# Feature-major loads of x with token moments broadcast through DRAM, in a two-layer float32 kernel

## The reference

```python
xn = _layernorm(x, axis=-1)                       # (x - mean) / sqrt(var + eps), per token
s = xn @ (weight * block_mask).T + bias           # layer 0: masked linear, 512 x 512
inter = xn @ c1_w.T @ c2_w.T                      # rank 16, then 1792 columns
idx = argmax of each block of 32 columns
h = relu(w1[idx] . xn);  g = silu(h @ w2t[idx])   # only the picked rows count
x = x + s * g
xn = _layernorm(x, axis=-1)                       # layer 1
s = attention(xn) @ Wo + bo                       # one head of 128
g = silu(xn @ base_w.T + base_b + top-2 LoRA experts of xn)
x = x + s * g
```

## Time and profile before

| what | value |
|---|---|
| median of 3 runs | 650.63 us (649.14 to 651.12) |
| the profiled execution | 650.05 us, of which the span of the profile is 648.2 us |
| TensorE busy | 632.3 us, 98% |
| VectorE busy | 446.3 us, 69% |
| ScalarE, GpSimd busy | 213.4 us, 240.0 us |
| granted TensorE clock | 0.999 of full speed |

### The profile page before, as it was taken

How to read it: one execution, slowest core, us unless ns; L and a number is a source line. 1 busy time by engine, 2 the same in 40 slices (tenths; PEclk the granted TensorE clock), 3 DMA queues, 4 the chain that set the end, 5 groups by cost and what they waited for, 6 DMA issues and landing times.

```text
span 648.2 us, 8466 instructions
## 1 busy us (share of the span) xinstructions
PE 632.3 (98%) x2942; PEld 509.9 (79%) x2942; DVE 446.3 (69%) x716; ACT 213.4 (33%) x379; POOL 240.0 (37%) x188
## 2 busy tenths in 40 slices
PE   7999999999999999999999999999999999999997
PEld 3768787878888878888878787778878878887887
DVE  7987776787765777765777886655765857575633
ACT  3533333312223312223322243651255035314510
POOL 2355545650000740000742644582425433351441
PEclk9999999999999999999999999999999999999999
DMA  9940000022400022300153622050140013012000
GB/s 282 400 158 1 2 0 1 26 81 52 127 17 9 26 81 70 108 16 8 32 141 95 173 82 73 17 178 1 49 147 1 16 50 129 0 41 89 2 32 33
DMA packets 42575, 46.16 MB, mean 71 GB/s; under 512 B 25072, under 2 KB 25456, under 8 KB 41904
## 3 DMA queue, kind: packets, MB, share of 16 engines
q1 hardware_dynamic: 42544, 45.76, 22.1%
HBM read 31.85 MB, written 8.39 MB: 62 GB/s over the span
## 4 chain that ended last, share of the span: by engine, by line
PE 81%; DVE 12%; issue 3%; ACT 1%; POOL 1%; DMA 1%; DVEq 0%; POOLq 0%; ACTq 0%; SPq 0%
PE bank L418 73%; DVE counts L940 3%; PE bank L348 2%; DVE seg_top L926 2%; DVE eq L928 2%; PE bank L1205 1%; PE bank L1359 1%; DMA first<-counts 1%; PE bank L1183 1%; DVE h_lo L970 1%; PE bank L1322 1%; DVE h L961 1%; POOL g_tile L394 1%; PE bank L1224 1%; DVE ws_raw L994 0%
## 5 line engine op out<-in xcount | busy, mean ns | idle before, releaser
L418 PE MATMUL bank<-w_hi_t,h_hi 128*128 128x512 f32 x224 | 90.4, 404 | 0.7 <-DVE h_lo L970 0.4
L761 ACT ACTIVATE h_hi<-h 128x512 fp32r<-128x512 f32 x56 | 35.4, 633 | 162.9 <-DVE h L961 162.9
L418 PE MATMUL bank<-w_lo_t,h_hi 128*128 128x512 f32 x224 | 87.6, 391 | 0.0
L418 PE MATMUL bank<-xT_hi,w_hi_t 128*128 128x512 f32 x224 | 87.4, 390 | 0.1
L418 PE MATMUL bank<-w_hi_t,h_lo 128*128 128x512 f32 x224 | 87.4, 390 | 0.0
L418 PE MATMUL bank<-xT_hi,w_lo_t 128*128 128x512 f32 x224 | 87.2, 389 | 0.0
L418 PE MATMUL bank<-xT_lo,w_hi_t 128*128 128x512 f32 x224 | 87.1, 389 | 0.0
L940 DVE TENSOR_TENSOR_SCAN counts<-restart,eq 128x512 bf16<-128x512 bf16 (+1 forms) x56 | 76.0, 1357 | 2.4
L394 POOL TENSOR_TENSOR g_tile<-g_tile,s_tile 128x512 f32<-128x512 f32 x31 | 44.3, 1430 | 88.3 <-DVE g_tile L983 44.2
L926 DVE TENSOR_REDUCE seg_top<-bank 128x16 f32<-128x512 f32 (+1 forms) x64 | 39.5, 617 | 46.2 <-PE bank L1205 46.2
L672 POOL TENSOR_TENSOR prod_lo<-prod,prod_hi 128x512 fp32r<-128x512 f32 x32 | 40.6, 1291 | 57.9 <-ACT prod_hi L801 57.8
(11 more groups left out here) (191 smaller groups left out, 1300.5 us busy)
## 6 DMA issues: line engine op xcount, KB each, us to landing
w_raw<-in_w SPq DMA_DIRECT2D x28, 256.0 KB, 10.1
x_res<-in_x SPq DMA_DIRECT2D x4, 1024.0 KB, 8.5
mid_state<-g_tile SPq DMA_DIRECT2D x16, 256.0 KB, 2.1
x_tile<-mid_state SPq DMA_DIRECT2D x4, 1024.0 KB, 7.4
x_res<-mid_state SPq DMA_DIRECT2D x4, 1024.0 KB, 5.5
out<-g_tile SPq DMA_DIRECT2D x15, 256.0 KB, 2.0
x_tile<-in_x SPq DMA_DIRECT2D x3, 1024.0 KB, 5.6
b_raw<-in_lora_b SPq DMA_DIRECT2D x2, 1024.0 KB, 5.1
```

Of the source, the lines that this page charges most:

```text
L418: last = nc.tensor.matmul(dst, a, b, start=(start and n == 0), stop=(stop and n == len(mms) - 1))
L761: nc.scalar.activation(h_hi[:, it % 2, :], h[:], ACT.Copy).then_inc(h_hi_done, 1)
```

## The change

For the second to fourth chunk of layer 0, `x_tile` is loaded from a second copy of x that the host lays out with features on the partitions. TensorE's transposes at the first three seams are gone. Statistics are still computed with tokens on partitions: each 128-token tile is loaded once more, one at a time, into a new tile `row` (which lies over layer 1's `comb` and its neighbours), and `bn_stats` reads it there, at `it` = 1, 3, 5, 7; `bn_aggr` follows at `it` = 8. SyncE writes mean and rstd to DRAM, 512 numbers each, by two stores of single elements, waits for both, and reads each back as one row broadcast to all partitions, the mean into `bias_b`, the rstd into `row`. VectorE then normalizes with two tensor-tensor instructions for each of the four feature blocks (`turned_norm`), the first block at `it` = 10, the second at 11, the last two at 12. The loads of `base_b` and `bqkv_col`, and the clearing of `comb`, move behind the last use of these tiles. `rank_product` waits for each feature block apart. GpSimd's program is the same.

```diff
+        def turned_stats(dve, g, tt):
+            dve.wait_ge(ld_row, ((g - 1) * TT + tt + 1) * 16)
+            nc.vector.bn_stats(bn[:, tt, :], row[:]).then_inc(stats_in, 1)
+        def turned_norm(dve, g, k):
+            dve.wait_ge(ld_moments, g * 2 * 16)
+            dve.wait_ge(ld_x, g * 16 + 16)
+            nc.vector.tensor_tensor(x_tile[:, k, :], x_tile[:, k, :], bias_b[:], ALU.subtract).then_inc(shifted, 1)
+            dve.wait_ge(shifted, (g - 1) * KD + k + 1)
+            nc.vector.tensor_tensor(x_tile[:, k, :], x_tile[:, k, :], row[:], ALU.mult).then_inc(xn_ready, 1)
+        def turned_hi(act, g, k):
+            act.wait_ge(xn_ready, g * KD + k + 1)
+            nc.scalar.activation(xT_hi[:, k, :], x_tile[:, k, :], ACT.Copy).then_inc(xT_hi_done, 1)
+        def turned_lo(dve, g, k):
+            dve.wait_ge(xT_hi_done, g * KD + k + 1)
+            nc.vector.tensor_tensor(xT_lo[:, k, :], x_tile[:, k, :], xT_hi[:, k, :].bitcast(F32), ALU.subtract).then_inc(xT_done, 1)
...
+            def next_row(c, tt):
+                if tt:
+                    sp.wait_ge(stats_in, (c + 1) * TT + tt)
+                else:
+                    sp.wait_ge(xn_ready, c * TT + TT)
+                sp.dma_start(row[:], x_rows[c + 1][:, tt, :]).then_inc(ld_row, 16)
+            def next_moments(c):
+                sp.wait_ge(rstd_step, c * 2 + 4)
+                with nc.allow_non_contiguous_dma(reason="one column for each tile"):
+                    sp.dma_start(moments_of[0], mean_var[:, :, 0]).then_inc(st_moments, 16)
+                    sp.dma_start(moments_of[1], rstd[:]).then_inc(st_moments, 16)
+                sp.wait_ge(st_moments, c * 32 + 32)
+                sp.dma_start(bias_b[:], moments[0:1, :].to_broadcast([P, S])).then_inc(ld_moments, 16)
+                sp.dma_start(row[:], moments[1:2, :].to_broadcast([P, S])).then_inc(ld_moments, 16)
...
                 for tt in range(TT):
                     turn(c, 3, tt)
+                    if not last and tt == 0:
+                        next_moments(c)
...
-            next_rows(0, x_rows[1])
+            next_row(0, 0)
+            next_rows(0, x_turned[1])
+            for tt in range(1, TT):
+                next_row(0, tt)
+            next_moments(0)
...
-                    if IT - 8 <= it < IT - 4:
+                    if last and IT - 8 <= it < IT - 4:
                         rows_stats(dve, c + 1, it - (IT - 8))
+                    if not last and it in (1, 3, 5, 7):
+                        turned_stats(dve, c + 1, it // 2)
...
-                    if it == IT - 4:
+                    if it == (IT - 4 if last else 8):
                         rows_moments()
-                    if it == IT - 2:
+                    if last and it == IT - 2:
                         rows_norm(dve, c + 1)
+                    if not last and IT - 4 <= it < IT - 1:
+                        turned_norm(dve, c + 1, it - (IT - 4))
+                    if not last and it == IT - 2:
+                        turned_norm(dve, c + 1, KD - 1)
...
+                if not last:
+                    pe.wait_ge(h_split, c * IT + IT)
+                    down_product(IT - 1, range(TT)).then_inc(down_done, 1)
+                    return
...
+        "x_turned": x.transpose(0, 2, 1).reshape(x.shape[0], KD, P, -1).transpose(0, 2, 1, 3),
```

More of the change, by code:

```diff
@@ L507, in chunk @@
                     turn(c, 1, tt)
+                    if not last and tt % 2:
+                        next_row(c, 1 + tt // 2)
                 sp.wait_ge(ld_first[TT - 1], (c * PIECES + 2) * 16)
@@ L513, in chunk @@
                     sp.dma_start(bias_a[:], bo.rearrange("(a n) -> a n", a=1).to_broadcast([P, D])).then_inc(ld_bo, 16)
+                    sp.wait_ge(xn_ready, CH * TT)
+                    sp.dma_start(bias_b[:], base_b.rearrange("(a n) -> a n", a=1).to_broadcast([P, D])).then_inc(ld_l1_small, 16)
+                    with nc.allow_non_contiguous_dma(reason="three short columns"):
+                        sp.dma_start(bqkv_col[:], bqkv.rearrange("(j p) -> p j", p=P)).then_inc(ld_l1_small, 16)
                 for tt in range(TT):
                     turn(c, 2, tt)
+                    if not last and tt == 1:
+                        next_row(c, 3)
                     if last and tt == 0:
```

62 lines of the change are left out of this document (43 added, 19 removed).

## The result

The changed kernel takes **680.64 us** (median of 5 runs, 679.92 to 681.78) against 650.63 (649.14 to 651.64), a ratio of 1.0465 (95% interval 1.045 to 1.0479): 30 us slower, where 12.7 were forecast and 672 was the end of the range. The profiled execution took 681.78, span 680.0.

A forecast was written before the change was run, and what follows sets the result against it. TensorE, busy 98% of the span, was taken as the bound, with the seams deciding. 14.7 + 0.4 - 2.2 = +12.9 on 650.05 gave 663.0, stated as 663.3 us for the median; range 659.5 to 672.

The forecast's parts named there:

- T = R + 8.1: Path through DRAM: both broadcast rows land (T) 8.1 us after rstd ends (R).
- T is in time by 1.8 us: Later seams: broadcast rows land at 195.1, VectorE wants them at 196.3 with 0.6 to spare; no wait.
- The stores: Path through DRAM: 1.7 us issue for each store; the second lands some 3.3 us after it starts.
- The broadcasts: Path through DRAM: two row broadcasts behind the stores take 0.5 + 2.5, counted as 3.1 us.
- The first seam: First to second chunk: VectorE stalls 17.8 us for the moments; rank product 14.7 us later, plus 0.4 for the clock.
- the clock's 0.4: First seam: down_product(11) alone runs at half clock after TensorE's idle, 5.4 us, adding 0.4 us.
- Rank product at T + 15.85: First seam: rank product starts 15.85 us after both broadcast rows land, at 132.85.
- The later seams: Second to third and third to fourth chunk: 1.1 us gained at each, -2.2 in all.
- The gain: Later seams: up to 2.06 us of transposes removed, 0.97 new stall before down_product(13), leaving 1.1 us gained each.
- stays low through the seam: Rival, first seam: three products of 5.4 us at low clock, +5.8 instead of +0.4, 668.7 us; 10%.
- The long path: Rival: path through DRAM takes 11 to 12 us, delaying all three seams, +21, 671.5 us; 15%.
- Elsewhere: Fourth seam, moved loads, clearing of comb and layer 1's next x_tile request: nothing for all.

The follow-up runs named there:

- e9: Changed kernel with small probe transfers behind its last store, each waited for alone; 512 side-by-side single values landed in 9.6 us.
- e2: Changed kernel with both moment stores in 16-byte runs (four neighbouring tokens per partition, mean copied to be contiguous); 661.05 us, ratio 1.0167.
- e4: Changed kernel with both moment stores issued twice, the extra pair first and to a spare tensor; 681.06 us, one execution.
- e5: Changed kernel with GpSimd making the first chunk's rstd ahead of its last weight parts and bias additions; 661.26 us, ratio 1.0165.
- e8: Changed kernel with the edits of e2 and e5 together; 649.15 us, ratio 0.9986 to the kernel before.
- e10: Changed kernel unaltered, run again beside e11; 678.04 us, ratio 1.0436.
- e12: e8 with subtraction and multiplication of the last two feature blocks moved from VectorE to GpSimd; 646.09 us, ratio 0.9942.
- e11: Changed kernel with 24 matmuls into an unread bank ahead of down_product(11) in chunks two and three; 678.18 us, ratio 1.043.
- e7: Changed kernel with all four subtract and multiply pairs at it = 12; 676.04 us, ratio 1.0406.

## Why the prediction was wrong

The direction, the place and the mechanism were right: VectorE waits for `ld_moments` with TensorE's next products queued behind it. What failed is one term, **"T = R + 8.1"**, with the step that rested on it, **"T is in time by 1.8 us"**.

- **The stores.** Predicted 1.7 of issue and 3.3 to landing, 5.0 in all. Measured 9.4, 13.05 and 9.46 us from the first issue to the first broadcast in the three chunks. The split was wrong as well: issue took 0.4 to 0.5 us (once 1.39), not 1.7. I had scaled the issue of `bqkv_col` by its element count and set its 9.8 us to landing aside as a full queue. That row is a load, though, and e9 reads 512 single values in 2.1 us with 0.37 of issue; in the changed kernel `bqkv_col` itself, with fewer loads ahead of it, is issued in 0.47. So the queue it stood in is the likely source of both of the row's numbers, as I had argued for the landing and not for the issue, and its nearness to 9.0 is chance. No row of before has a scattered write, and I priced one as if it were a scattered read.
- **The page's rule.** The Trainium skill, "DMA: Bandwidth & Descriptors", Rules for kernel authors, says to rearrange a non-contiguous last dimension. Following it (e2, 16-byte runs) gave back 17 to 20 us, so the trace agrees with the advice. But its reason, a descriptor for each element, isn't what costs here: e9's values 64 bytes apart are single elements too and land in 2.4. The same page's Specifications say that a transfer below 512 bytes is done as read-modify-write. That could be why neighbouring writes hold each other up (9.6 us), but by itself it would make the values 64 and 512 bytes apart and the 16-byte runs slow too, and they take 2.4, 1.8 and 1.4.
- **The broadcasts.** Predicted 3.1 from first issue to both landed, measured 124.43 - 119.27 = 5.2, 4.5 and 5.6: some two microseconds more. In e9 one broadcast alone takes 3.4, in e2 the two take 3.4 and 3.8 and 4.2 together. Standing behind single-value stores is not what slows them (4.5 and 4.8 here), since behind twice as many, in e4, they take 3.2 and 3.7. The cause is open.
- **The first seam.** Predicted +14.7 and +0.4, measured +21.0. T - R brought 6.5 more, R stood 0.2 earlier, the clock's 0.4 did not come: 15.1 + 6.5 - 0.2 - 0.4 = 21.0. "Rank product at T + 15.85" was right, 15.80. So was R, and that GpSimd's order makes it late: e5 takes 17 us back out of R, and 20 of the 24 us of stall with it. The 0.4 stood for a `down_product(11)` of 5.4 us; it took 5.1 (129.39 to 134.47), which the time that TensorE would have waited ahead of `down_product(13)` just covers.
- **The later seams.** Predicted -1.1 each, measured +6.55 and +3.07. The prediction had VectorE wanting T at R + 9.3; it was 17.6 and 15.0 behind R, less waits of 8.14 and 5.62, which is 9.4 each time. So the slack was read rightly and T was not. For the second seam the wait closes the account: from the end of `h_lo` at `it` = 10 to the rank product before, 213.81 - 196.40 = 17.41 us; after, 8.14 + 15.82 = 23.96; the difference is 6.55. At the third the same sum gives 5.62 + 15.78 - 17.41 = 3.99 where 3.07 was lost. The other 0.9 lies ahead of the wait, in the head of the third chunk: the kernel before takes 21.82 us there from rank product to first mask multiply, the changed one 20.99, and VectorE's first scan in it, beside GpSimd, takes 2.32 us before and 1.45 after. Nothing in it waits for the moments.
- **The gain.** 1.1 us a seam, with 0.97 of new stall ahead of `down_product(13)`: e8 has 1.0 and 0.75 at the second seam, and 2.1 us over the two later seams from rank product to rank product. Right, and it needs the path to be short before it can be seen.
- **The clock.** The rival "stays low through the seam" did not occur: the granted clock was 0.58 from 130 to 135 us and 1.00 from 135 on. By "TensorE: Matmul & The Clock Gate", Part 1, of the Trainium skill the clock returns after some microseconds of matmuls; the trace agrees, half speed at 129 (rows 0.43 us apart) and full at 135. This rival's own terms, three products of 5.4 from T + 5.0, end at T + 21.2, not 21.6.
- **The rivals and the range.** The long path (15%) had T - R = 11 to 12 and gave 671.5; the real one was longer. Its ceiling took 9.8 for both stores and 2.6 for both broadcasts, so 12.4, against 14.6, 17.6 and 15.0: the stores of the second chunk alone took 12.6 us to land. With these three in place of 8.1 the prediction's own arithmetic gives 14.7 + 6.5 at the first seam and, with its 0.6 to spare and its gain of 1.1, 7.7 - 1.1 and 5.1 - 1.1 at the later ones: 21.2, 6.6 and 4.0 against the measured 21.0, 6.55 and 3.07. The model was sound, its one unmeasured input not. (The forecast's last step rounds: 12.9 on the median of 650.63 is 663.5, not 663.3.)
- **Elsewhere.** Predicted nothing, measured 0.1 behind the last rank product. The 1.1 us ahead of the first one aren't the change's: e10, the same kernel, starts it at 15.44 as before. In the first profile the granted clock was 0.66 from 10 to 15 us, in e10 1.00.

## What to carry to other kernels

A wait for a transfer that stands in the order of a busy engine costs the whole path behind it, so that path needs a price of its own: a scattered write can't be priced by a plain transfer, nor by a scattered read, and where no row has one, the forecast's range has to stay open above. Where values that different partitions hold must go to DRAM side by side, let each partition own neighbouring ones and write them as one run; it was a change of an index pattern and a copy of 128x4 values here, and worth 17 us or more. And when an operand is wanted earlier than before, look at the program order of whoever makes it: the change left GpSimd's as it was, and mending that alone was worth as much (17 to 19 us).

## What the runs showed of the hardware that I had not expected

- Single 4-byte writes to DRAM side by side from different partitions: 9.6 us for 512 of them, 8.1 for 128, against 2.4 for 512 values 64 bytes apart, 1.8 for 512 bytes apart and 1.4 in runs of 16 bytes. Two such stores together end at 9.9, the last three of four in a kernel at 9.9 to 10.1. Reading 512 single values takes 2.1. The DMA engines are busy for two of these microseconds only, and idle until the landing.
- Its landing is 7.5 to 9.0 us at most seams in the kernels, but 11.3 to 12.6 for the second of two stores at the second seam, wherever the path is used at all three.
- Issuing such a store takes 0.4 to 0.5 us, and 1.0 to 1.4 for that same store at the second seam. The count of elements doesn't show in it: 512 single values read back need 0.37 of issue, where `bqkv_col` with 384 had 1.29.
- VectorE's tensor-tensor instructions on 128x512 take 1.0 to 1.8 us beside GpSimd's on such tiles, 0.69 alone (e8, e12); the mask multiply of the first chunk, with one input in a bank, takes 0.69 beside them too (e12 at 107.83). GpSimd doing half of the normalization pays in spite of it.
- The same fall of the clock to 1.2 GHz was free where another engine's chain ended last (e10, e11) and cost 2.5 us where the slow product was the last of the seam (e7).
